# Four-layer graph network on one core: products with the edge means made early and kept, biases added on VectorE

## What is computed

```python
h = relu(layernorm(x)); x = x + L0(h)    # attention, 4 heads, then gelu([out, h] @ W1.T + b1) @ W2.T + b2
h = relu(layernorm(x)); x = x + L1(h)    # two rounds, edge_attr is 100000 x 64
h = relu(layernorm(x)); x = x + L2(h)    # one round
h = relu(layernorm(x)); x = x + L3(h)    # attention, 8 heads, then a feed-forward part with b1, b2
...
# L1: both rounds use the same mean of the edge attributes
nbr_r = segment_sum(h_r, dst) * inv_deg
def layer(h, W, b):
    nbr_x = segment_sum(h[src], dst) * inv_deg
    return relu(concatenate([h, nbr_x, nbr_r], axis=1) @ W + b)
h = layer(h_e, W1, b1); h = layer(h, W2, b2)
# L2
x = concatenate([h[tgt], h[src] - h[tgt]], axis=-1)
y = where(cnt > 0, segment_sum(x @ W.T + b, tgt) / max(cnt, 1), 0)
```

## Time and profile before

| | before |
|---|---|
| median of 3 runs | 6147.66 us (6140.43 to 6149.96) |
| the profiled execution: its time | 6139.35 us |
| the profiled execution: its span | 6137.6 us |
| PE busy | 2661.9 us (43%) |
| DVE busy | 4092.7 us (67%) |
| ACT busy | 1253.9 us (20%) |
| POOL busy | 3783.2 us (62%) |
| mean granted clock of TensorE | 0.604 |

### The profile page before, as it was taken

One profiled execution on the slowest core, in us unless ns is written; L12 is line 12 of the kernel. 1 busy time (PEld: TensorE's weight loads), 2 busy tenths in 40 slices (PEclk: granted clock), 3 DMA queues, 4 the chain that ended last, 5 costly groups with the idle time before them and its releaser, 6 DMA issues.

```text
span 6137.6 us, 56339 instructions
## 1 busy us (share of the span) xinstructions
PE 2661.9 (43%) x13332; PEld 1809.3 (29%) x13333; DVE 4092.7 (67%) x6865; ACT 1253.9 (20%) x4370; POOL 3783.2 (62%) x3760
## 2 busy tenths in 40 slices
PE   1785101011332322222222342677674577777746
PEld 0661101011322222222222242546453232332315
DVE  9778888886986776767676774232322576676655
ACT  0000000000111111111111110000000677777741
POOL 2777777776777777777777774000002777777730
PEclk6555555555555555555555555767685788888876
DMA  6221121211222222222222231435261222332230
GB/s 229 53 54 51 48 56 48 73 29 50 77 79 61 72 61 71 63 70 64 69 64 68 66 85 39 144 104 179 69 205 22 58 83 77 87 86 77 84 98 7
DMA packets 388365, 472.44 MB, mean 77 GB/s; under 512 B 212478, under 2 KB 248384, under 8 KB 381041
## 3 DMA queue, kind: packets, MB, share of 16 engines
q1 hardware_dynamic: 132624, 279.73, 13.8%
q0 software_dynamic: 114832, 129.82, 9.7%
q10 hardware_dynamic: 140752, 61.28, 3.5%
HBM read 291.34 MB, written 179.19 MB: 77 GB/s over the span
## 4 chain that ended last, share of the span: by engine, by line
POOL 58%; issue 21%; PE 9%; DMA 6%; DVE 5%; ACT 0%; POOLq 0%; DVEq 0%; ACTq 0%; SPq 0%
POOL arena L738 44%; POOL rec_dram L695 11%; PE acc L1959 4%; DMA oh<-mt_dram 2%; PE acc L1780 2%; DMA V<-in_edge_attr_dram 2%; DMA rec_dram<-V,rowst 1%; PE acc L1782 1%; PE acc L1943 1%; POOL own_dram L715 1%; POOL pdum L688 1%; POOL arena L765 1%; DVE arena L1579 1%; PE pt L1770 0%; POOL own_dram L769 0%
## 5 line engine op out<-in xcount | busy, mean ns | idle before, releaser
L738 POOL DMA_INDIRECT arena<-tab_dram,jst x2592 | 2685.8, 1036 | 778.3 <-issue 777.8
L695 POOL DMA_INDIRECT rec_dram<-V,rowst x784 | 866.1, 1105 | 229.9 <-issue 217.8
L688 POOL TENSOR_TENSOR pdum<-pdum 128x1 f32<-128x1 f32 x197 | 58.5, 297 | 1138.3 <-DVE arena L1607 864.6
L1902 PE MATMUL pw<-OHX 128*128 128x128 bf16 x1632 | 210.3, 310 | 1120.8 <-DVE OHX L1414 1120.8
L1902 PEld LDWEIGHTS pw<-OHX 128*128 128x128 bf16 x1632 | 156.9, 140 | 1172.3 <-DVE OHX L1414 859.7
L1910 PE MATMUL acc<-arena,oh 128*128 128x64 f32 x1952 | 427.1, 420 | 20.9 <-DVE oh L1423 20.7
L1910 PEld LDWEIGHTS acc<-arena,oh 128*128 128x128 f32 x1952 | 417.2, 330 | 34.9 <-issue 34.9
L900 ACT ACTIVATE arena<-arena,ew 128x64 f32<-128x64 f32 x1728 | 417.8, 333 | 33.3 <-PE acc L1983 33.3
L1437 DVE TENSOR_TENSOR arena<-arena,pt 128x1024 f32<-128x1024 f32 x108 | 131.8, 1221 | 431.7 <-DMA arena<-tab_dram,jst 429.4
L900 ACT ACTIVATE OHX<-arena,ew 128x64 f32<-128x64 f32 x1728 | 417.7, 333 | 2.5
L1983 PE MATMUL acc<-OHX,ident 128*128 128x512 f32 x432 | 253.7, 753 | 371.0 <-ACT OHX L900 371.0
(11 more groups left out here) (523 smaller groups left out, 6463.2 us busy)
## 6 DMA issues: line engine op xcount, KB each, us to landing
oh<-mt_dram SPq DMA_DIRECT2D x90, 512.0 KB, 3.6
arena<-tab_dram,jst POOLq DMA_INDIRECT x2592, 2.5
arena<-rec_dram SPq DMA_DIRECT2D x122, 288.0 KB, 3.6
mt_dram<-oh ACTq DMA_DIRECT2D x272, 128.0 KB, 1.7
oh<-mt_dram SPq DMA_DIRECT2D x75, 416.0 KB, 3.9
oh<-mt_dram SPq DMA_DIRECT2D x75, 384.0 KB, 4.0
rows_dram<-V SPq DMA_DIRECT2D x27, 1056.0 KB, 4.0
rows_dram<-arena SPq DMA_DIRECT2D x27, 1056.0 KB, 4.3
```

The lines of the kernel that those rows point to most:

```text
L695: gp.indirect_dma_start(rec[:, :], bass.IndirectOffsetOnAxis(ap=rowst[:, q, k:k + 1], axis=0), recst[:, q, k, :], None).then_inc(S[f"scat{ ...
L738: gp.indirect_dma_start(hd.G[:, a.r, j, :], None, table[:, :], row_of(jst[:, a.r, j:j + 1])).then_inc(S[f"{x}g{a.r}"], 16)
L1902: last = nc.tensor.matmul(unit_bank(c.slot)[:, k // 2 * P:(k // 2 + 1) * P], mones[c.slot][:, 0, k, :], mones[c.slot][:, 1, k, :], start=k ...
```

## The change

The part of L1's two products that uses `nbr_r` is computed once, in the time of the list-end gathers, and kept. PE transposes `nbr_r` there (into the bank pair `pw`, which ACT copies to `NRT`), makes both products, and DVE adds the round's bias to each while it moves them out of PSUM (`NBW[0]` and `NBW[1]`, 128 x 1600 each). In the rounds, PE makes the product with 25 matmuls, and DVE adds the kept array. The biases are now on all 128 partitions of `bias` (five loads of 128 x 64 in the place of 1 x 64), and no product has a bias matmul. `b2` of the first attention is added to `X` beside the gathers; that of the last product is added to `Hn` before DVE waits for PE. In each round the copy of `Hn` into `CAT` stands at the start, where it stood behind the sums.

```diff
         NRT = OHXf[0:D, 0:2 * NC * D]
+        NBW = [OHXf[:, k * NC * D:(k + 1) * NC * D].rearrange("p (c d) -> p c d", d=D) for k in (2, 3)]
         SUM3 = area(0, 3)
...
-        bias = sb("bias", [1, 5, D])
+        bias = sb("bias", [P, 5, D])
...
-                sp.dma_start(bias[:, k, :], t[name].unsqueeze(0)).then_inc(S["wts"], 16)
+                sp.dma_start(bias[:, k, :], t[name].unsqueeze(0).to_broadcast([P, D])).then_inc(S["wts"], 16)
...
-            def transposed(K, dst=None):
+            def transposed(K, dst=None, frm=pt):
...
-                    A.copy((T if dst is None else dst)[0:K, b * 512:b * 512 + m], pt[0:K, bank:bank + m]).then_inc(S["tc"], 1)
+                    A.copy((T if dst is None else dst)[0:K, b * 512:b * 512 + m], frm[0:K, bank:bank + m]).then_inc(S["tc"], 1)
...
-            def exponentials(x, bufs):
+            def exponentials(x, bufs, done=0):
                 for k, buf in enumerate(bufs):
-                    act.wait_ge(S[x + "cx"], k + 1)
+                    act.wait_ge(S[x + "cx"], done + k + 1)
                     A.activation(buf, buf, ACT.Exp).then_inc(S[x + "cb"], 1)
...
             first_attention(act, weights0)
-            exponentials("a", [CX0[1], CX0[2], FC0, FX0])
+            exponentials("a", [CX0[1], CX0[2], FC0])
+            transposed(D, NRT, pw)
+            exponentials("a", [FX0], 3)
             transposed(2 * D)
...
             transposed(2 * D)
-            transposed(D, NRT)
             transposed(2 * D)
...
             V.tensor_copy(FM, Mn).then_inc(S["afd"], 1)
+
+            def bias_of(k):
+
+                return bias[:, k, :].unsqueeze(1).to_broadcast([P, NC, D])
+            v.wait_ge(S["lin"], 3)
+            V.tensor_tensor(NBW[0], acc_n, bias_of(1), ALU.add).then_inc(S["act"], 1)
+            v.wait_ge(S["act"], 3)
+            link(V.tensor_tensor(X[:], X[:], bias_of(0), ALU.add))
+            v.wait_ge(S["lin"], 4)
+            link(V.tensor_tensor(NBW[1], acc_n, bias_of(2), ALU.add))
             v.wait_ge(S["aeg"], 2 * NC * 16)
...
             V.tensor_copy(CAT[:, :, D:2 * D], Hn[:]).then_inc(S["ev"], 1)
-            v.wait_ge(S["lin"], 3)
+            v.wait_ge(S["lin"], 5)
             link(V.tensor_tensor(X[:], X[:], acc_n, ALU.add))
...
             for r in range(3):
+                link(V.tensor_copy(CAT[:, :, 0:D], Hn[:]))
+
                 def take_chunk(a):
...
                 v.wait_ge(S["cadd"], (r + 1) * ADDS)
-                link(V.tensor_copy(CAT[:, :, 0:D], Hn[:]))
                 link(V.tensor_reduce(XC, SUM3.rearrange("p (c k d) -> p c d k", k=3, d=D), AX, ALU.add))
...
                 V.memset(vdum[:, 0:1], 0.0).then_inc(S["ev"], 1)
-                v.wait_ge(S["lin"], 4 + r)
+                v.wait_ge(S["lin"], 6 + r)
+                link(V.tensor_tensor(XC, acc_n, NBW[r] if r < 2 else bias_of(3), ALU.add))
                 if r == 0:
-                    link(V.tensor_scalar(Hn[:], acc_n, 0.0, None, ALU.max))
+                    link(V.tensor_scalar(Hn[:], XC, 0.0, None, ALU.max))
                     split_rows()
...
                 if r == 1:
-                    link(V.tensor_scalar(XC, acc_n, 0.0, None, ALU.max))
+                    link(V.tensor_scalar(XC, XC, 0.0, None, ALU.max))
                 else:
-                    link(V.tensor_tensor(XC, acc_n, hasin[:].unsqueeze(2).to_broadcast([P, NC, D]), ALU.mult))
+                    link(V.tensor_tensor(XC, XC, hasin[:].unsqueeze(2).to_broadcast([P, NC, D]), ALU.mult))
                 link(V.tensor_tensor(X[:], X[:], XC, ALU.add))
...
-            v.wait_ge(S["lin"], 7)
+            v.wait_ge(S["lin"], 9)
             link(V.tensor_copy(AS[:], acc[:, 0:NC * 2 * H3].rearrange("p (c h) -> p c h", h=2 * H3)))
...
             V.memset(vdum[:, 0:1], 0.0).then_inc(S["ev"], 1)
-            v.wait_ge(S["lin"], 8)
-            link(V.tensor_tensor(Hn[:], Hn[:], acc_n, ALU.add))
+            link(V.tensor_tensor(XC, Hn[:], bias_of(4), ALU.add))
+            v.wait_ge(S["lin"], 10)
+            link(V.tensor_tensor(Hn[:], XC, acc_n, ALU.add))
             norm(Hn[:], Hn[:], 3, 4)
...
-            def transposes(src, K):
+            def transposes(src, K, into=pt):
...
                     for j in range(min(4, NC - 4 * b)):
-                        last = nc.tensor.transpose(pt[0:K, bank + j * P:bank + (j + 1) * P], src[:, 4 * b + j, :], ident[:])
+                        last = nc.tensor.transpose(into[0:K, bank + j * P:bank + (j + 1) * P], src[:, 4 * b + j, :], ident[:])
                     last.then_inc(S["tp"], 1)
...
-            def product(parts, width, bk=None):
+            def product(parts, width):
...
                     for n, (TL, K, R) in enumerate(parts):
-                        last = nc.tensor.matmul(o, TL[0:K, c * P:(c + 1) * P], R, start=n == 0, stop=n == len(parts) - 1 and bk is None)
-                    if bk is not None:
-                        last = nc.tensor.matmul(o, ones[0:1, :], bias[:, bk, :], start=False, stop=True)
+                        last = nc.tensor.matmul(o, TL[0:K, c * P:(c + 1) * P], R, start=n == 0, stop=n == len(parts) - 1)
                 last.then_inc(S["lin"], 1)
...
             last.then_inc(S["acp"], 1)
+            transposes(nbr_r[:], D, pw)
+            for k in range(2):
+                if k:
+                    pe.wait_ge(S["act"], 3)
+                product([(NRT, D, W1b[:, k, :])], D)
             pe.wait_ge(S["ev"], 3)
...
             hidden(WT[:, 2, :], 2 * D, 0)
-            product([(T2, D, WT[0:D, 3, :])], D, 0)
+            product([(T2, D, WT[0:D, 3, :])], D)
...
                 transposes(CAT, 2 * D)
-                if r == 0:
-                    transposes(nbr_r[:], D)
-                if r < 2:
-                    product([(T, 2 * D, W1a[:, r, :]), (NRT, D, W1b[:, r, :])], D, 1 + r)
-                else:
-                    product([(T, 2 * D, WT[:, 4, :])], D, 3)
+                product([(T, 2 * D, W1a[:, r, :] if r < 2 else WT[:, 4, :])], D)
...
             hidden(F1[:], D, 8)
-            product([(T2, 2 * D, F2[:])], D, 4)
+            product([(T2, 2 * D, F2[:])], D)
```

## The result

| | before | after |
|---|---|---|
| median, us | 6147.95 (6140.43 to 6149.96, 4 runs) | 5988.98 (5985.01 to 5992.55, 4 runs) |
| profiled execution, us | 6139.35 | 5990.28 |
| its span, us | 6137.6 | 5988.5 |
| PE busy, us | 2661.9 | 2541.3 |

The ratio is 0.9743, with a 95% interval of 0.9727 to 0.976. The forecast of 6003 was 14 us too high. The kernel became 159 us faster by the medians and 149.1 by the spans.

The account below looks back on a forecast made before the run. POOL's gathers and their gaps were taken to hold most of the span, PE 9%. Terms -140.7 - 5.6 + 3.9 + 1.0 = -141.4 gave 5998 to 6006, taken as 6003 us; range 5989 to 6030.

Parts of the forecast that it names:

- The price of a matmul: In the five PE products, matmuls with unchanging weight rows cost 0.24 us at clock 1.00 and 0.437 at 0.50.
- Rival 1: In the products, the gap isn't from alternating rows and stays: only 116.2 us saved there, time about 6027 us; chance 10%.
- The products: Five PE products shrink to 25 same-row matmuls each, saving 140.7 us in all, bounds 125.1 to 149.6.
- I take it that the clock falls at the same moments as now: In each product, 1.00 was assumed to last as before: 5.0, 6.0, 4.3, 3.9 and 0 us, then 0.50.
- The cover: Early transposes, products and adds hide beside the list-end gathers, costing +1.0 us (0 to 1.8); uncovered, 30 us.
- Rival 2: Early work draws out list-end gathers by 1.0 us each: 24 of them, 6027 us, or all 50, 6053 us; chance 4%.
- DVE: DVE work on the path: -5.6 us for copies moved, +3.9 (up to 5.6) for added instructions in the rounds.
- -5.6 for the copies: Copy of Hn leaves three round closes, 1.82 us and a 0.03 gap each, and hides at the round's start.
- The maximum: In rounds 0 and 1 it becomes its own DVE instruction of 0.99 us, adding 1.03 each, or 1.86 if slow.
- rival 3: In the attentions, the gap between POOL's gathers grows from 0.30 us; at 0.37, 181 us lost, 6179 us; chance 2%.
- The offset: Whole kernel: median 8.3 us above the profiled execution, open by 5 each way; 5998 or 6006, taken as 6003.
- The start: Five bias loads on 128 partitions make SP's queue 0.7 us later, absorbed by PE's wait: 0, at most 0.7.

Follow-up runs that it names:

- run 1: Changed kernel with one-row bias matmuls back behind each matmul of the five products; 7963.08 us on a slow chip, five stretches 230.1 us against 123.3.
- run 2: Changed kernel with bias matmuls back, each with as many weight rows as the product's own; 7876.8 us on a slow chip, ratio 0.9945.
- run 3: Changed kernel with one-row bias matmuls back in one block behind each product's weight matmuls, zero matmuls opening the accumulators; 6079.98 us against 5993.15.
- run 4: Changed kernel with edge means transposed and multiplied in the rounds again, biases still on DVE; slow chip, five stretches 167.0 us against 123.3.
- run 5: Changed kernel with the early transposes, products and adds held until all list-end gathers landed; slow chip, that stage 126.74 us instead of 92.83.
- run 7: Changed kernel with 12 more DVE adds beside the list-end gathers, one operand in PSUM; slow chip, gather stage 93.49 us.
- run 8: Changed kernel with the copies of Hn back behind the sums in each round; slow chip, the three round stretches 5.7 us longer in all.
- run 11: Changed kernel unedited, measured again on another chip of the fast kind; 5993.15 us, ratio 0.9752.
- run 12: Kernel before the change, unedited, profiled again on a slow chip; 7968.2 us.
- filler: Changed kernel with four unread small matmuls behind each matmul of the last hidden layer, or of both; with both 5987.98 us against 5993.15.
- run 6: Changed kernel with 12 more DVE adds beside the list-end gathers, both operands in SBUF; slow chip, gather stage 100.25 us.

## Why the prediction was right, and what in it was not

**The price of a matmul.** 0.24 at clock 1.00 and 0.437 at 0.50 were measured as 0.232 and 0.437. That the gap goes with the alternating rows is shown by runs 1, 2 and 3: the same matmuls cost 0.19 us less each when the neighbours have the same rows, and one row alone isn't slow. The Trainium skill, TensorEngine Tiling (Array Packing), Key Properties, says that a change of the tiling mode drains TensorE. The traces agree in that the gap comes and goes with the change of rows; that this change is one of the mode, or the gap a drain, no run shows. Rival 1 is refuted.

**The products.** The sum of -140.7 was measured as -140.9, with errors that cancel: W2 20.7 forecast and 18.1 measured, round 0 43.6 and 44.2, round 1 36.0 and 36.7, round 2 20.4 and 21.8, the last 20.0 and 20.1. The step that failed is "I take it that the clock falls at the same moments as now". In rounds 1 and 2 it did not fall at all (5.8 us instead of 7.4 and 7.8), and in W2's it fell sooner in this profile (9.0 instead of 6.8; 6.55 to 9.28 in nine profiles). Run 2 shows that in the rounds the fall had come with the alternation: 100 records with the same rows stay at 1.00 for 11.38 us in all three. Why it falls in W2's product, whose rows don't alternate, and in run 3 stays open. That the sum came out within 0.2 us is luck: equal products differ by more between profiles. Of 25 round products with 128 rows alone, in nine profiles, 22 were at 1.00 throughout and three at 0.64 to 0.66. So a single profile of this kernel moves by 3 us a product from this alone.

**How much each half is worth.** Of the 140.9, run 1 puts 106.8 to the biases and run 4 43.7 to the edge means, with an overlap of 9.6. Of the 106.8, run 2 gives 37.3 to the 125 matmuls themselves, and the other 69.5 to changing rows and the clock that goes with it. Left on TensorE but not alternating they would have cost 82 (run 3, with the zeros that open the accumulators, 4.1 us in round 0) or 37 (run 2).

**The cover.** The gather stage took +0.62 us, for a forecast of 1.0 from one gather drawn out to 1.94. In this profile it was drawn out to 1.48, but in the ten profiles that have the add to `X` beside the gathers it took 1.43 to 2.58 us, 2.00 on the mean, so 1.06 more than 0.94. The term and its bounds (0 to 1.8) were right, and the 0.4 too little is where this one gather happened to start. Rival 2 is refuted by runs 4, 5 and 7.

**DVE.** -5.6 for the copies is supported by run 8 (5.7). The maximum took 0.99. The whole group was -4.3 instead of -1.7: 1.7 of the difference is PE's product behind round 2, which took 6.98 us at clock 0.81 instead of 8.71 at 0.64, by the clock and not by the edit (the same code took 9.39 there in run 11). The last 0.9 is within what the rounds differ by among equal kernels.

**What no step names.** 4.1 us had gone before the change's first instruction, 3.8 of them inside the first attention (2221.14 us against 2224.90). Three more profiles with the changed code gave 2221.63, 2220.53 and 2219.75. The gathers are 2 to 4 ns shorter on average there (1050 before, 1046 to 1048 after, 1631 of them), which accounts for 2.6 to 5.6 us. It isn't rival 3's mechanism: that was the gap between gathers, which stood still (489.5 us in all before, 489.4 after). Nor do the runs support an effect of the edit on the gathers. All 1728 of the first attention took 1817.1 us before and 1810.1 to 1813.2 in the four profiles with the changed code on short chips, but 1806.8 in run 12, with the kernel before, against 1807.6 to 1814.9 on that chip with the changed code. So it looks like a difference between executions; that it was one in the first profile isn't shown.

**The offset.** The sum against the profiled execution was 5998, and 5990.28 came: 3.8 of the error is the attention, 2.6 DVE's group, 0.4 the gathers, and the rest is spread. The 8.3 between the profiled execution and the median was carried over in part; in the changed kernel the profiled execution lies 1.3 above the median. The place of one execution among the others is chance, and the 5 us added for it should have been left out.

**The start** cost 0, as forecast: the first attention begins at 1521.80 us against 1522.19. PE's busy time fell by 120.6 us for 114.

## What to carry to other kernels

A small matmul that only adds a bias isn't free because it is small: look at the steps between starts in the trace, and where neighbours differ in rows, give them the same rows, or move the bias to an engine that takes the accumulator anyway. Compute early what depends on nothing late, in a stretch where the trace shows the engines idle behind a queue, and let what VectorE does there beside gathers read PSUM rather than two operands in SBUF. A mean clock of a stretch tells how much of it ran at which level, but not that the same moments would be slow after a change: price products at both levels and keep both for the range.

## What was unexpected in the hardware

In the rounds, alternating row counts cost more through the clock than through the gap: in round 0 of run 1 the 100 records took 28.04 us at a mean clock of 0.57, in run 2 11.38 at 1.00. At equal clock the gap alone is 9.3 us at 0.50 (the last product) and, from steps of 0.37 and 0.232, an estimated 6.9 at 1.00.

Of 25 products behind identical transposes 22 ran at 1.00 and three at 0.64 to 0.66; while the last product, the same 50 records behind a hidden layer, had 0.50 to 0.58 in every profile without filler, though PE is busy for 14.58 of the 16.0 us ahead of it, and even where the clock had been 0.83 to 0.88 in the stretch ahead.

In run 6 the gathers fell into step with the adds: ten in a row took 1.54 to 2.14 us, and from the second on one started every 1.86 us, as the adds do, instead of every 1.25. So in a stream of such adds the price is 0.61 us an add, while a single add costs a gather anything from nothing to 1.64 us.

The same program took 1800 us more on two of the chips. The trace of the kernel before there has waits that the first has not: PE waited 996 us in 169 times for nothing that the profile shows, by the view of waits (columns: engine, line, what was waited for, us in total, times, longest):

```profile
ACT oh L866 <- remote: 1367.6, 92, 35.4
...
PE pw L1902 <- issue: 996.1, 169, 22.3
```

On the first chip the same line of PE waits for DVE's `OHX` instead, 1120.8 us in 200 times. The product stretches agree (table above), and the gathers of both attentions last 1024 to 1029 ns on the mean there against 1034 to 1036. What it is stays open.
